# Second attention: the causal mask of a diagonal tile's row maximum, added by VectorE in the PSUM bank instead of by TensorE products

## The chip, the cores and the metric

One core of one Trainium2 chip runs the whole kernel. The metric is the device time of one execution in microseconds (us), the median of three runs. The program works on five engines that wait for each other through semaphores: TensorE (PE, with its weight loads PEld), VectorE (DVE), ScalarE (ACT), GpSimd (POOL) and SyncE (SP).

## What is computed

The reference has two layers, each an attention `s` times a gate `silu(g)`, added to `x`. The change is in the attention of the second layer, a causal softmax over 2048 positions with 16 heads of 64:

```python
scores = jnp.einsum('bqhd,bkhd->bhqk', q, k) / jnp.sqrt(jnp.float32(D_HEAD))
causal = jnp.tril(jnp.ones((seq, seq), dtype=bool))
scores = jnp.where(causal, scores, -jnp.inf)
pattern = jax.nn.softmax(scores, axis=-1)
z = jnp.einsum('bhqk,bkhd->bqhd', pattern, v)
attn_out = jnp.einsum('bqhd,hdm->bqm', z, W_O) + b_O
```

The softmax subtracts from each row an estimate of its maximum before the exponential. This maximum has to be taken over the columns that the causal mask leaves, and it is this mask that the change moves.

## The kernel before, in words

`attention1` works on 8 pairs of heads; the two heads of a pair lie in the lower and upper 64 partitions, called m = 0 and 1. For a pair, the queries are cut in 4 chunks of 512 columns (qc) and the keys in 16 tiles of 128 (kt). The main work is a list of 320 steps (pair, qc, kt) with kt up to the diagonal, so 4, 8, 12 and 16 steps for the four chunks of a pair, 40 for a pair. Four steps make a **group**, ten groups a **lap** (one pair).

All products that another engine has to read out go through **units**: a ring of RING = 3 places of two PSUM banks each. `UNIT` is the one hand-written order of all units, and TensorE, ScalarE and VectorE each walk it:

- `scores`: one step, a transposed 128 x 512 tile of scores for both heads. Six products for the scores in two precisions (L1788) and two that add minus the row maximum (L1791). ScalarE takes the exponential into `prob` (L1895) and so frees the place.
- `maximum`: one tile of 128 query rows i by up to 512 keys (chunk c), for the row maximum alone: one product per head, q_hi by k_hi (L1731). VectorE reduces it along the free axis into `part_max` (L1952), 128 x (2 x n) elements to 128 x 2, and so frees the place. There are 40 such tiles per pair, 320 in all; 16 per pair, 128 in all, are **diagonal** (c == i // 4) and are n = 128, 256, 384 or 512 columns wide per head, four of each per pair. In those the last 128 columns need the mask. Before, TensorE adds it: four products per tile (L1736, two per head, in bf16, 128 columns each) of an identity with a mask table, into the same bank.
- `project`, `value`, `turn`, `mix`: the projections of q, k and v for the next pair, the turn of the maxima into a row, and the output product. `turn` needs the maxima of its whole chunk (`neg_max`, L1960).

TensorE may fill the place of unit n only when unit n - 3 is freed (`room_for`). A group is: its rows phase (`rows_phase`: mostly a maximum, a scores, a maximum, a scores and so on, by the tables MAXIMA and PLACES), its whole phase (`whole_phase`: one to three of the other units), a `total` of the sums where a chunk has ended, and then the four `weigh` (L1810, prob by v, eight products, into a bank of their own), which need no place in the ring. VectorE walks the same units, and after a chunk has ended it also does `scale` (L1973 a reciprocal of 128 x 512, L1976 a product), behind the units of the group and ahead of those of the next. The maxima are computed ahead of the scores that need them: the first pair's in the start and groups 0 to 4, the others' in the 70 groups after that (seven equal laps), and the last five groups have none.

Where two VectorE instructions depend on each other, `link` (class Chain) makes the later wait on a semaphore that the earlier one raises at its end.

The mask table and the identity are made by GpSimd in `second_constants`, during the first attention.

Of the kernel before, what the change touches and what calls it, by code (L numbers as in the profile page):

```python
# [9 lines left out]
BF16 = mybir.dt.bfloat16  # L10
I32 = mybir.dt.int32
ALU = mybir.AluOpType
# [3 lines left out]
P = 128  # L16
# [3 lines left out]
C = 512  # L20
NC = S // C
TC = C // P
# [21 lines left out]
HD1 = 64  # L44
# [3 lines left out]
NEG = -1e30  # L48
# [344 lines left out]
def join_result(nc, link, sh, c, x_done):  # L393

    at = slice(c * TC, (c + 1) * TC)
    for t in range(c * TC, (c + 1) * TC):
        last = nc.gpsimd.tensor_scalar(sh.xa[:, t, 0:D], sh.xa[:, t, 0:D], sh.rstd[:, 0, t:t + 1],  # L397
                                       sh.shift[:, 0, t:t + 1], ALU.mult, ALU.add)
    link(last)
    link(nc.gpsimd.tensor_tensor(sh.xa[:, at, 0:D], sh.xa[:, at, 0:D], sh.g[:, at, :], ALU.mult))  # L400
    nc.gpsimd.tensor_tensor(sh.x[:, at, :], sh.x[:, at, :], sh.xa[:, at, 0:D], ALU.add).then_inc(x_done, 1)
# [30 lines left out]
def attention0(nc, a, sh):  # L432

    with ExitStack() as ctx:
# [7 lines left out]
        RING = 3  # L442
# [55 lines left out]
        @block.sync  # L498
        def _(sp):

            load_rows(sp, sh, 2, q_rows[2], k_rows[2], rows_loaded[2])
            load_rows(sp, sh, 3, q_rows[3], k_rows[3], rows_loaded[3])
            sp.dma_start(sh.w_out[:, :], a["L0_attn_w_out"]).then_inc(sh.join_loaded, 16)
            for n, name in enumerate(("b_out", "gamma", "beta")):
                sp.dma_start(sh.rows[:, n, :], a["L0_attn_" + name].partition_broadcast(P)).then_inc(sh.join_loaded, 16)
            for n, name in enumerate(("w_gate", "w_up")):
                sp.dma_start(sh.w_int[:, n, :].rearrange("p (t d) -> p t d", d=D),
                             a["L1_ffn_" + name].rearrange("(t p) d -> p t d", p=P)).then_inc(sh.join_loaded, 16)
            sp.dma_start(sh.w_int[:, 2, :], a["L1_ffn_w_down"]).then_inc(sh.join_loaded, 16)
            load_heads_start(sp, a, sh)  # L510

        @block.gpsimd
        def _(pool):
            link = Chain(pool, fold_step)

            def row(n):
                return sh.rows[:, n:n + 1, :].to_broadcast([P, T, D])

            for group in range(1, G):
                nc.gpsimd.memset(v_cols[group][:, :, :, HD0 + 1:VW], 0.0)  # L520
                nc.gpsimd.memset(v_cols[group][:, :, :, HD0:HD0 + 1], 1.0)
                heads = sh.v0[:, :, group * GH * HD0:(group + 1) * GH * HD0]
                nc.gpsimd.tensor_copy(v_cols[group][:, :, :, 0:HD0],
                                      heads.rearrange("p t (h j) -> p t h j", j=HD0)).then_inc(v_copied, 1)

            pool.wait_ge(sh.join_loaded, 16 * 7)
            link(nc.gpsimd.tensor_tensor(beta_g, sh.g[:, :, :], row(2), ALU.mult))
            link(nc.gpsimd.tensor_tensor(sh.x[:, :, :], sh.x[:, :, :], beta_g, ALU.add))
            link(nc.gpsimd.tensor_tensor(sh.g[:, :, :], sh.g[:, :, :], row(1), ALU.mult))
            link(nc.gpsimd.tensor_tensor(sh.xa[:, :, 0:D], sh.xa[:, :, 0:D], row(0), ALU.add))  # L530
            pool.sem_inc(folded, 1)

            second_constants(nc, link, sh, sh.xnT)

            for c in range(NC - 1):
                pool.wait_ge(scaled, 2 * c + 1)
                join_result(nc, link, sh, c, x_done)
                pool.wait_ge(scaled, 2 * c + 2)
                join_normal(nc, sh, c, normed)
# [921 lines left out]
                multiply(3, f)  # L1461


def second_constants(nc, link, sh, scratch):

    HALF = [slice(0, HD1), slice(HD1, 2 * HD1)]
    for m in range(2):
        masks = scratch[:, m * C:(m + 1) * C].rearrange("p (k h c) -> p k h c", k=2, h=2)
        link(nc.gpsimd.memset(masks, 0.0))
        link(nc.gpsimd.affine_select(out=masks[:, 0, :, :], in_=masks[:, 0, :, :], compare_op=ALU.is_ge,  # L1470
                                     fill=NEG, base=-m * HD1, pattern=[[HD1, 2], [-1, P]], channel_multiplier=1))
        link(nc.gpsimd.affine_select(out=masks[:, 1, :, :], in_=masks[:, 1, :, :],
                                     compare_op=ALU.not_equal, fill=1.0, base=-m * HD1,
                                     pattern=[[HD1, 2], [-1, P]], channel_multiplier=1))
        nc.gpsimd.tensor_copy(sh.causal[HALF[m], :, :], masks[HALF[m], 0, :, :])
        link(nc.gpsimd.tensor_copy(sh.ident_b[HALF[m], :, :], masks[HALF[m], 1, :, :]))
    nc.gpsimd.memset(sh.ones_r[:, :].bitcast(F32), 1.0)
    link(nc.gpsimd.memset(sh.own_tile[:, :, :], 0.0))
    for m in range(2):
        link(nc.gpsimd.affine_select(out=sh.own_tile[:, :, :], in_=sh.own_tile[:, :, :], compare_op=ALU.not_equal,  # L1480
                                     fill=1.0, base=-m * HD1, pattern=[[-1, TC], [0, P]], channel_multiplier=1))
# [15 lines left out]
def attention1(nc, a, sh, out):  # L1497

    with ExitStack() as ctx:
# [6 lines left out]
        W = HD1  # L1506
        HALF = [slice(0, W), slice(W, 2 * W)]
        NP = H // 2
        PR = 6
        RING = 3  # L1510
# [60 lines left out]

            return hp * NC + c

        wo, row_o, causal, ident_b, ones_r, own_tile = sh.wo, sh.row_o, sh.causal, sh.ident_b, sh.ones_r, sh.own_tile
        bias = sb("bias", [P, 3, NP])
        q_hi = sb("q_hi", [P, S], F32R)
        q_lo = sb("q_lo", [P, S], F32R)
        k_hi = [sb(f"k_hi{n}", [P, S], F32R) for n in range(2)]
# [37 lines left out]
        unit_both = [sh.psum[:, 2 * r:2 * r + 2, :] for r in range(RING)]  # L1616
# [84 lines left out]
        def _(pe):  # L1701
# [21 lines left out]
            def maximum(hp, i, c):  # L1723
                to = room_for(("maximum", hp, (i, c)))
                if c == 0 and i % TC == 0:

                    pe.wait_ge(act_split, (nth("project", hp, i // TC) + 1) * 2)
                n = min(C, (i + 1) * P - c * C)
                diagonal = c == i // TC
                for m in range(2):  # L1730
                    last = nc.tensor.matmul(to[:, m, 0:n], q_hi[HALF[m], i * P:(i + 1) * P],  # L1731
                                            k_hi[hp % 2][HALF[m], c * C:c * C + n], start=True, stop=not diagonal)
                if diagonal:
                    for half in range(2):
                        for m in range(2):
                            last = nc.tensor.matmul(to[:, m, n - P:n], ident_b[HALF[m], half, :],  # L1736
                                                    causal[HALF[m], half, :], start=False, stop=half == 1)
                last.then_inc(unit_filled, 1)

            def turn_maxima(hp, c):  # L1740
# [89 lines left out]
            for m in range(3):  # L1830
                last = nc.tensor.transpose(out_bank[:, m * NP:(m + 1) * NP], sh.bias_rows[:, m * P:(m + 1) * P],
                                           sh.ident[0:NP, 0:NP])
# [7 lines left out]
            for n in range(NP):  # L1840
                last = nc.tensor.matmul(side_bank[:, 0:D], bias_v[:, n, :], wo[:, n, :],
                                        start=n == 0, stop=n == NP - 1)
# [82 lines left out]
        def _(dve):  # L1925
            link = Chain(dve, result_step)
# [21 lines left out]
            def reduce_tile(hp, i, c):  # L1948
                n = AT["maximum", hp, (i, c)]
                cols = min(C, (i + 1) * P - c * C)  # L1950
                dve.wait_ge(unit_filled, n + 1)
                nc.vector.tensor_reduce(part_max[:, :, i, c], unit_both[n % RING][:, :, 0:cols], AX_X, ALU.max)\  # L1952
                    .then_inc(unit_freed[n % RING], 1)
                if (i + 1) % TC == 0 and c == i // TC:

                    tiles = [u for u in TILES if u[1] == hp and u[2][0] // TC == c]
                    for r in range(RING):
                        for u in [u for u in tiles if AT[u] % RING == r][-1:]:
                            wait_freed(dve, u)
                    nc.vector.tensor_reduce(neg_max[:, c % 2, :, 0:TC], part_max[:, :, c * TC:(c + 1) * TC, 0:c + 1],  # L1960
                                            AX_X, ALU.max, negate=True).then_inc(max_done, 1)
# [118 lines left out]
def build(nc, a, out):  # L2080
    with ExitStack() as ctx:
        sh = Shared()

        def sb(name, shape, dt=F32):
            return ctx.enter_context(nc.sbuf_tensor(name, shape, dt))
# [8 lines left out]
        sh.x_high, sh.x_low = (sb(name, [P, S], F32R) for name in ("x_high", "x_low"))  # L2094
        sh.wo = sb("wo", [P, H // 2, D])
        sh.row_o = sb("row_o", [P, D])
        sh.causal, sh.ident_b = (sb(name, [P, 2, P], BF16) for name in ("causal", "ident_b"))
        sh.ones_r = sb("ones_r", [P, P], F32R)
        sh.own_tile = sb("own_tile", [P, TC, P])
        sh.bias_rows = sb("bias_rows", [H // 2, 3 * P])  # L2100
# [62 lines left out]
```

## Time and profile before

| | before |
|---|---|
| median of 3 runs | 1413.13 us (1411.38 to 1413.79) |
| profiled execution | 1410.19 us |
| its span, first to last instruction | 1408.2 us |
| mean granted TensorE clock | 0.982 |
| busy: PE / DVE / ACT / POOL | 93% / 72% / 53% / 49% |
| second attention, from the start of the span | from about 548 us to the end |

The profile is one execution, seen by the hardware profiler. A line's busy time counts overlapping instructions once, the mean is that of one instruction. In a timeline each row is a run of equal instructions on one engine: start, length, engine, line, what is written from what, shape, count, and in brackets the idle time before it and whose end ended it. The products of the two heads of a unit run side by side in the halves of the array, so a pair of products of 512 columns starts every 0.23 us and not every 0.46.

### The profile page before, as it was taken

How to read it: one execution, taken by the hardware profiler on the slowest of the kernel's cores; microseconds unless marked ns; L12 is line 12 of the kernel's file. 1: busy time of each engine (PE TensorE's matmuls, PEld its weight loads, DVE VectorE, ACT ScalarE, POOL GpSimd, SP SyncE). 2: the span in 40 equal slices, each digit the busy share in tenths (PEclk: the TensorE clock that was granted, in tenths of full speed). 3: DMA queues.
4: the chain of work that ended last, by engine and by line, in shares of the span. 5: the costliest groups of instructions: out<-in, count | busy, mean ns of one | idle time of the engine just before them, and what ended most of it. 6: DMA issues, size and time to landing. Idle time of an engine off the chain costs nothing.

```text
span 1408.2 us, 25489 instructions
## 1 busy us (share of the span) xinstructions
PE 1313.0 (93%) x9902; PEld 674.9 (48%) x9902; DVE 1015.9 (72%) x1495; ACT 749.8 (53%) x1200; POOL 691.9 (49%) x527
## 2 busy tenths in 40 slices
PE   5778999999999987989999999999999999999897
PEld 3654222222222245555555655555555555555554
DVE  7666888888888875776766766766766666766768
ACT  5275777877777774334444444444344344344343
POOL 4301060100100010558678678677677677777671
PEclk9799999999999999999999999999999999999999
DMA  2511320000000000000000000000000000000000
GB/s 98 160 74 51 111 47 1 1 1 1 2 1 2 2 1 1 1 1 1 1 1 1 1 1 1 1 1 0 1 1 1 1 1 1 1 1 1 1 16 16
DMA packets 18166, 21.50 MB, mean 15 GB/s; under 512 B 7785, under 2 KB 15873, under 8 KB 16513
## 3 DMA queue, kind: packets, MB, share of 16 engines
q1 hardware_dynamic: 18048, 19.88, 4.6%
q8 instruction: 81, 1.33, 0.4%
q14 instruction: 37, 0.30, 0.1%
HBM read 14.63 MB, written 5.24 MB: 14 GB/s over the span
## 4 chain that ended last, share of the span: by engine, by line
PE 43%; DVE 11%; ACT 3%; issue 1%; POOL 1%; DVEq 0%; POOLq 0%; ACTq 0%
PE psum L1810 13%; PE psum L1788 12%; DVE part_max L1952 4%; PE psum L1731 4%; DVE inv L1973 4%; PE psum L1791 3%; ACT prob L1895 3%; PE psum L1769 2%; PE psum L1718 2%; PE psum L1757 2%; PE psum L1709 1%; DVE z L1976 1%; PE psum L1711 1%; PE psum L1710 1%; PE psum L1736 1%
## 5 line engine op out<-in xcount | busy, mean ns | idle before, releaser
L1698 POOL TENSOR_TENSOR acc<-acc,prob 128x1024 f32<-128x1024 f32 (+3 forms) x250 | 492.8, 1971 | 87.4 <-ACT prob L1895 57.6
L1895 ACT ACTIVATE prob<-psum 128x1024 f32<-128x1024 f32 (+1 forms) x320 | 283.3, 897 | 353.8 <-PE psum L1791 346.4
L1952 DVE TENSOR_REDUCE part_max<-psum 128x2 f32<-128x1024 f32 (+2 forms) x320 | 336.7, 1063 | 170.0 <-PE psum L1731 85.6
L696 DVE TENSOR_SCALAR w<-psum 128x512 f32<-128x512 f32 x472 | 304.7, 686 | 59.0 <-PE psum L553 46.6
L647 ACT ACTIVATE w<-psum 128x512 f32<-128x512 f32 x552 | 294.2, 600 | 85.4 <-PE psum L553 84.8
L573 PE MATMUL psum<-w,v_cols 128*32 128x512 f32 x2048 | 274.1, 608 | 0.0
L1810 PE MATMUL psum<-prob,v_pair 128*64 128x512 f32 (+3 forms) x1280 | 250.2, 532 | 0.7 <-POOL prob L1666 0.7
L1788 PE MATMUL psum<-q_hi,k_hi 64*128 64x512 f32 (+3 forms) x640 | 139.0, 430 | 30.4 <-DVE part_max L1952 21.5
L1810 PEld LDWEIGHTS psum<-prob,v_pair 128*64 128x64 f32 x1280 | 87.4, 137 | 145.2 <-issue 134.2
L1731 PE MATMUL psum<-k_hi,q_hi 64*128 64x512 f32 (+3 forms) x640 | 132.5, 411 | 6.0 <-DVE part_max L1952 4.4
L1788 PE MATMUL psum<-q_lo,k_hi 64*128 64x512 f32 (+3 forms) x640 | 119.1, 368 | 0.0
L1788 PE MATMUL psum<-q_hi,k_lo 64*128 64x512 f32 (+3 forms) x640 | 119.1, 368 | 0.0
L1791 PE MATMUL psum<-max_rows,ones_r 64*128 64x512 f32 (+3 forms) x640 | 118.7, 366 | 0.0
L1973 DVE RECIPROCAL inv<-psum 128x512 f32<-128x512 f32 x31 | 103.9, 3352 | 16.5 <-PE psum L1757 16.5
L553 PEld LDWEIGHTS psum<-q_rows,k_rows 32*128 32x128 f32 x768 | 40.3, 181 | 154.0 <-ACT w L647 148.1
L397 POOL TENSOR_SCALAR xa<-xa,rstd_j,shift_j 128x128 f32<-128x128 f32 x16 | 6.9, 449 | 209.0 <-DVE shift_j L389 209.0
L1666 POOL TENSOR_SCALAR_AFFINE_SELECT prob<-prob 128x256 f32<-128x256 f32 x128 | 53.3, 423 | 110.9 <-ACT prob L1895 110.1
L553 PE MATMUL psum<-q_rows,k_rows 32*128 32x512 f32 x768 | 101.6, 493 | 0.1
L1788 PEld LDWEIGHTS psum<-q_hi,k_hi 64*128 64x128 f32 x640 | 61.4, 188 | 78.0 <-DVE part_max L1952 47.4
L1731 PEld LDWEIGHTS psum<-k_hi,q_hi 64*128 64x128 f32 x640 | 61.2, 187 | 77.6 <-issue 40.8
L1694 POOL TENSOR_TENSOR acc<-prob 128x1024 f32<-128x1024 f32 x23 | 54.9, 2385 | 43.2 <-ACT prob L1895 41.4
L573 PEld LDWEIGHTS psum<-w,v_cols 128*32 128x32 f32 x2048 | 40.6, 108 | 63.8 <-ACT w L647 53.5
(301 smaller groups left out, 1411.3 us busy)
## 6 DMA issues: line engine op xcount, KB each, us to landing
q_rows<-q_dram SPq DMA_DIRECT2D x12, 256.0 KB
k_rows<-k_dram SPq DMA_DIRECT2D x3, 1024.0 KB
q_dram<-parts SPq DMA_DIRECT2D x2, 1024.0 KB, 4.2
k_dram<-parts SPq DMA_DIRECT2D x2, 1024.0 KB, 6.6
x<-in_L_attn_x SPq DMA_DIRECT2D x4, 256.0 KB, 4.0
mask<-in_L_ffn_attention_mask SPq DMA_DIRECT2D x1, 1024.0 KB, 6.0
x_high<-q_dram SPq DMA_DIRECT2D x4, 256.0 KB
x_low<-k_dram SPq DMA_DIRECT2D x1, 1024.0 KB
```

The lines of the kernel that those rows point to most:

```text
L553: last = nc.tensor.matmul(pair_bank[n % RING][i], k_rows[group][rows, kt * P:(kt + 1) * P], q_rows[group][rows, qc * C:(qc + 1) * C], star ...
L573: last = nc.tensor.matmul(out_bank[turn % 2][h * VW:(h + 1) * VW, :], v_cols[group][:, kt, h, :], w[:, s % WR, h, :], start=(kt == 0), sto ...
L647: nc.scalar.activation(w[:, s % WR, 2 * m + i, :], pair_bank[n % RING][i], ACT.Relu)\
L696: nc.vector.tensor_scalar(w[:, s % WR, 2 * m + 1, :], pair_bank[n % RING][1], 0.0, None, ALU.max)\
L1698: nc.gpsimd.tensor_tensor(sums, sums, prob[:, s % PR, :, q0:C], ALU.add).then_inc(summed, 1)
L1731: last = nc.tensor.matmul(to[:, m, 0:n], q_hi[HALF[m], i * P:(i + 1) * P], k_hi[hp % 2][HALF[m], c * C:c * C + n], start=True, stop=not di ...
L1788: nc.tensor.matmul(to[:, m, q0:C], left[HALF[m], keys], right[HALF[m], at], start=n == 0, stop=False)
L1791: last = nc.tensor.matmul(to[:, m, q0:C], ones_r[HALF[m], :], max_rows[HALF[m], at], start=False, stop=True)
L1810: last = nc.tensor.matmul(out_bank[HALF[m], q0:C], v_pair[hp % 2][:, kt, HALF[m]], prob[:, s % PR, m, q0:C], start=kt == 0, stop=kt == (qc ...
L1895: nc.scalar.activation(prob[:, s % PR, :, q0:C], unit_both[n % RING][:, :, q0:C], ACT.Exp, scale=SCALE)\
L1952: nc.vector.tensor_reduce(part_max[:, :, i, c], unit_both[n % RING][:, :, 0:cols], AX_X, ALU.max)\
L1973: nc.vector.reciprocal(inv[:, :], side_bank).then_inc(inv_done, 1)
```

## The change

The four mask products of a diagonal tile (L1736) are gone; the tile's two products then close their accumulation themselves. In their place VectorE, when it comes to a diagonal tile, first adds a mask of 128 x 128 f32 (zero, or -1e30 above the diagonal) to the last 128 columns of both banks, in place in PSUM, for both heads in one instruction, waits for its end through `link`, and then runs the reduce as before. The mask table is one f32 tile in place of two pairs of bf16 ones, and the identity is gone; `second_constants` has a memset and a select in place of ten instructions.

```diff
-def second_constants(nc, link, sh, scratch):
...
+    link(nc.gpsimd.memset(sh.causal[:, :], 0.0))
+    link(nc.gpsimd.affine_select(out=sh.causal[:, :], in_=sh.causal[:, :], compare_op=ALU.is_ge, fill=NEG, base=0,
+                                 pattern=[[-1, P]], channel_multiplier=1))
...
                 for m in range(2):
                     last = nc.tensor.matmul(to[:, m, 0:n], q_hi[HALF[m], i * P:(i + 1) * P],
-                                            k_hi[hp % 2][HALF[m], c * C:c * C + n], start=True, stop=not diagonal)
-                if diagonal:
-                    for half in range(2):
-                        for m in range(2):
-                            last = nc.tensor.matmul(to[:, m, n - P:n], ident_b[HALF[m], half, :],
-                                                    causal[HALF[m], half, :], start=False, stop=half == 1)
+                                            k_hi[hp % 2][HALF[m], c * C:c * C + n], start=True, stop=True)
...
                 dve.wait_ge(unit_filled, n + 1)
+                if c == i // TC:
+                    own = unit_both[n % RING][:, :, cols - P:cols]
+                    link(nc.vector.tensor_tensor(own, own, causal[:, :].unsqueeze(1).to_broadcast([P, 2, P]), ALU.add))
                 nc.vector.tensor_reduce(part_max[:, :, i, c], unit_both[n % RING][:, :, 0:cols], AX_X, ALU.max)\
                     .then_inc(unit_freed[n % RING], 1)
...
-        sh.causal, sh.ident_b = (sb(name, [P, 2, P], BF16) for name in ("causal", "ident_b"))
+        sh.causal = sb("causal", [P, P])
```

On VectorE, around the end of chunk 3 of a pair's scores (groups 16 and 17), the instructions stood in this order before (the reduces of `maximum` units are `part_max<-psum`; x5 means five in a row):

```order
L1960 TENSOR_REDUCE neg_max<-part_max 128x2x4
L1952 TENSOR_REDUCE part_max<-psum 128x2 x3
L1941 SCALAR_TENSOR_TENSOR k_lo0<-psum,bias,k_hi0 128x512
L1944 SCALAR_TENSOR_TENSOR q_lo<-psum,bias,q_hi 128x512
L1973 RECIPROCAL inv<-psum 128x512
L1976 TENSOR_TENSOR z<-z,inv 128x512
L1952 TENSOR_REDUCE part_max<-psum 128x2 x5
```

and so they stand now:

```order
L1949 TENSOR_REDUCE neg_max<-part_max 128x2x4
L1941 TENSOR_REDUCE part_max<-psum 128x2
L1940 TENSOR_TENSOR psum<-psum,causal 128x2x128
L1941 TENSOR_REDUCE part_max<-psum 128x2 x2
L1927 SCALAR_TENSOR_TENSOR k_lo0<-psum,bias,k_hi0 128x512
L1930 SCALAR_TENSOR_TENSOR q_lo<-psum,bias,q_hi 128x512
L1962 RECIPROCAL inv<-psum 128x512
L1965 TENSOR_TENSOR z<-z,inv 128x512
L1940 TENSOR_TENSOR psum<-psum,causal 128x2x128
L1941 TENSOR_REDUCE part_max<-psum 128x2 x2
L1940 TENSOR_TENSOR psum<-psum,causal 128x2x128
L1941 TENSOR_REDUCE part_max<-psum 128x2 x2
```

Each diagonal tile has one add more, straight ahead of its reduce, and one of them stands directly behind the reciprocal and product of `scale`.

On TensorE, at the end of group 14 (tiles of query rows 15 by keys of chunk 3), the order was

```order
L1791 MATMUL psum<-max_rows,ones_r 128x512 x2
L1731 MATMUL psum<-k_hi0,q_hi 128x512 x2
L1736 MATMUL psum<-causal,ident_b 128x128 x4
L1709 MATMUL psum<-x_high,w_high 128x512
L1710 MATMUL psum<-x_low,w_high 128x512
```

and is now

```order
L1777 MATMUL psum<-max_rows,ones_r 128x512 x2
L1722 MATMUL psum<-k_hi0,q_hi 128x512 x2
L1701 MATMUL psum<-x_high,w_high 128x512
L1702 MATMUL psum<-x_low,w_high 128x512
```

The four mask products have gone, and nothing else has moved.

## Rows read from the trace of the kernel before

**Rows 1.** The page: busy time by engine, and one group of GpSimd.

```profile
PE 1313.0 (93%) x9902; PEld 674.9 (48%) x9902; DVE 1015.9 (72%) x1495; ACT 749.8 (53%) x1200; POOL 691.9 (49%) x527
...
L397 POOL TENSOR_SCALAR xa<-xa,rstd_j,shift_j 128x128 f32<-128x128 f32 x16 | 6.9, 449 | 209.0 <-DVE shift_j L389 209.0
```

**Rows 2.** Stretches: from:to, length, engines' busy us (instructions), clock, DMA share, GB/s.

```profile
717.50:822.50 105.00, 101.09 (x735) 60.11 (x733) 69.71 (x69) 45.22 (x56) 79.60 (x54) 0.98 0.00 1
822.50:926.30 103.80, 99.88 (x736) 59.03 (x734) 69.86 (x70) 45.19 (x56) 79.42 (x54) 1.00 0.00 1
...
794.70:798.10 3.40, 3.40 (x18) 2.50 (x16) 2.03 (x3) 1.97 (x2) 2.15 (x1) 0.51 0.00 0
```

**Rows 3.** Groups by line and shape, 520 to 1408: busy us, mean ns | idle before.

```profile
L1952 DVE TENSOR_REDUCE part_max<-psum 128x2 f32<-128x1024 f32 x224 | 272.2, 1223 | 93.6 <-PE psum L1731 85.6 <-PE psum L1736 6.7
...
L1736 PE MATMUL psum<-causal,ident_b 64*128 64x128 bf16 x512 | 36.9, 222 | 0.0
...
L1967 DVE TENSOR_TENSOR max_rows<-psum,own_tile 128x512 fp32r<-128x512 f32 x32 | 21.8, 682 | 13.5 <-PE psum L1743 13.5
...
L1952 DVE TENSOR_REDUCE part_max<-psum 128x2 f32<-128x256 f32 x32 | 13.6, 425 | 17.4 <-PE psum L1736 15.9
```

**Rows 4.** Who waited for whom, whole span: us in total, times, longest us.

```profile
PEld psum L1788 <- DVE part_max L1952: 47.4, 80, 2.3
```

**Rows 5.** Timeline of group 14 behind the end of a chunk, DVE and PE.

```profile
717.38 3.35 DVE L1973 RECIPROCAL inv<-psum 128x512 f32<-128x512 f32 x1
...
720.77 0.69 DVE L1976 TENSOR_TENSOR z<-z,inv 128x512 f32<-128x512 f32 x1
...
721.38 2.08 DVE L1952 TENSOR_REDUCE part_max<-psum 128x2 f32<-128x768 f32 x2
...
722.38 0.50 PE L1788 MATMUL psum<-q_hi,k_hi 64*128 64x512 f32 x2 [0.93 <-DVE part_max L1952]
```

**Rows 6.** Timeline of PE in groups 16 and 17.

```profile
740.58 0.41 PE L1731 MATMUL psum<-k_hi,q_hi 64*128 64x512 f32 x2
...
740.91 0.49 PE L1788 MATMUL psum<-q_hi,k_hi 64*128 64x512 f32 x2
741.23 0.41 PE L1788 MATMUL psum<-q_hi,k_lo 64*128 64x512 f32 x2
...
742.43 0.50 PE L1788 MATMUL psum<-q_hi,k_hi 64*128 64x512 f32 x2
...
745.18 0.50 PE L1709 MATMUL psum<-x_high,w_high 128*128 128x512 f32 x1
...
756.21 0.39 PE L1731 MATMUL psum<-k_hi,q_hi 64*128 64x512 f32 x2
756.44 0.41 PE L1788 MATMUL psum<-q_hi,k_hi 64*128 64x512 f32 x2
756.69 0.40 PE L1788 MATMUL psum<-q_hi,k_lo 64*128 64x512 f32 x2
```

**Rows 7.** Timeline of DVE in groups 16 and 17.

```profile
739.81 0.96 DVE L1952 TENSOR_REDUCE part_max<-psum 128x2 f32<-128x768 f32 x1 [2.12 <-PE psum L1736]
741.15 1.23 DVE L1952 TENSOR_REDUCE part_max<-psum 128x2 f32<-128x1024 f32 x1 [0.39 <-PE psum L1736]
...
742.50 1.78 DVE L1952 TENSOR_REDUCE part_max<-psum 128x2 f32<-128x1024 f32 x2
...
752.91 0.68 DVE L1952 TENSOR_REDUCE part_max<-psum 128x2 f32<-128x512 f32 x1
```

**Rows 8.** Timeline of DVE in group 11, behind the end of a chunk.

```profile
688.44 1.21 DVE L1952 TENSOR_REDUCE part_max<-psum 128x2 f32<-128x1024 f32 x1
```

**Rows 9.** Timeline of DVE at the start of the second attention.

```profile
553.13 3.01 DVE L1952 TENSOR_REDUCE part_max<-psum 128x2 f32<-128x256 f32 x4
...
558.84 0.29 DVE L2050 TENSOR_TENSOR row_o<-row_o,psum 128x128 f32<-128x128 f32 x1 [1.23 <-PE psum L1841]
```

**Rows 10.** Timeline of PE in group 21, one lap after group 11.

```profile
793.59 0.50 PE L1788 MATMUL psum<-q_hi,k_hi 64*128 64x512 f32 x2 [1.87 <-DVE part_max L1952]
```

More of the change, by code:

```diff
@@ L531, in _ @@
             pool.sem_inc(folded, 1)
-            second_constants(nc, link, sh, sh.xnT)
+            second_constants(nc, link, sh)
             for c in range(NC - 1):
@@ L1461, in _, with second_constants @@
                 multiply(3, f)
-def second_constants(nc, link, sh, scratch):
-    HALF = [slice(0, HD1), slice(HD1, 2 * HD1)]
-    for m in range(2):
[L1468 to L1476, printed above, removed]
+def second_constants(nc, link, sh):
+    link(nc.gpsimd.memset(sh.causal[:, :], 0.0))
+    link(nc.gpsimd.affine_select(out=sh.causal[:, :], in_=sh.causal[:, :], compare_op=ALU.is_ge, fill=NEG, base=0,
+                                 pattern=[[-1, P]], channel_multiplier=1))
     nc.gpsimd.memset(sh.ones_r[:, :].bitcast(F32), 1.0)
@@ L1572, in nth @@
             return hp * NC + c
-        wo, row_o, causal, ident_b, ones_r, own_tile = sh.wo, sh.row_o, sh.causal, sh.ident_b, sh.ones_r, sh.own_tile
+        wo, row_o, causal, ones_r, own_tile = sh.wo, sh.row_o, sh.causal, sh.ones_r, sh.own_tile
         bias = sb("bias", [P, 3, NP])
@@ L1728, in maximum @@
                 n = min(C, (i + 1) * P - c * C)
-                diagonal = c == i // TC
                 for m in range(2):
                     last = nc.tensor.matmul(to[:, m, 0:n], q_hi[HALF[m], i * P:(i + 1) * P],
-                                            k_hi[hp % 2][HALF[m], c * C:c * C + n], start=True, stop=not diagonal)
-                if diagonal:
-                    for half in range(2):
-                        for m in range(2):
-                            last = nc.tensor.matmul(to[:, m, n - P:n], ident_b[HALF[m], half, :],
-                                                    causal[HALF[m], half, :], start=False, stop=half == 1)
+                                            k_hi[hp % 2][HALF[m], c * C:c * C + n], start=True, stop=True)
                 last.then_inc(unit_filled, 1)
```

## The prediction

> **What bounds the kernel now.** The page comes first: TensorE is busy in 93% of the span and VectorE in 72% [rows 1], so a change that takes work from the one and gives it to the other looks like a gain. The stretches say the same of a single lap: in 103.80 us TensorE is busy 99.88 and VectorE 69.86 [rows 2]. But the busy share hides latencies: a matmul's row counts its pass through the array. The waits must be read. The weight loads of the scores waited 47.4 us in 80 places for VectorE's reduce of a maximum [rows 4], nearly all in the stretches where the work is passed to and fro through the ring of three places. And the timelines show the kind: a scores unit starts 0.05 us after the reduce three units before it has ended (reduce ends at 742.38, next scores at 742.43 [rows 6, 7]). So in a rows phase the time is often set by fill, reduce, fill, exponential, and only in the whole phase and the weigh by TensorE's own stream. What counts is which diagonal tiles lie on that chain.
>
> **What TensorE saves.** The 512 mask products occupy 36.9 us [rows 3], 0.29 per tile, but they overlap their neighbours. What goes is read from starts. With a mask, from the tile's first product to the second pair of the scores behind it is 741.23 - 740.58 = 0.65 us; without one, in a stretch where nothing waits, 756.69 - 756.21 = 0.48 [rows 6]. So a tile gives back about 0.17 us, where TensorE is the last; 0.10 is the low end (the start alone: 740.91 - 740.58 = 0.33 against 0.23). For 128 tiles that is 13 to 22 us, if all were on the path. Where the unit behind the mask waits for the ring anyway, it gives nothing. Weighed against the trace, the Trainium skill (TensorE: Matmul & The Clock Gate, section "Back-to-back issue gap") has a stream of loads and products of 128 columns spaced about 81 ns apart, which would make four of them 324 ns a tile and the whole 41 us; the starts above are closer together, since the two heads' products run side by side.
>
> **What VectorE gains in work.** One add of 128 x 256 elements, PSUM and SBUF in, PSUM out. The trace has no such write to PSUM; the nearest rows are the add from PSUM and SBUF of 128 elements, 0.29 us [rows 9], and the product of 512, 682 ns [rows 3]: in between, 0.42 for 256, which is also what a reduce of 256 takes (425 ns [rows 3]). To that comes the wait of the reduce for the add: 0.04 us, as between the reciprocal (ends 720.73) and the product that waits for it (starts 720.77) [rows 5]. I take 0.46 per tile, 59 us in all. The ends: 0.40, and, if a write into PSUM cost as much again as the fixed part of the shortest row, 0.6. The skill says (VectorE: DVE Perf Modes, section "The DRAIN you can't avoid") that the semaphore costs nothing extra between chained instructions. Four reduces without a wait take 3.01 us for 0.43 + 0.69 + 0.96 + 1.22 = 3.30, that is, they overlap by about 0.1 [rows 9]; a waiting one does not. By the page's rule 0.14 us of each exposed add would go, some 6 us of the sum.
>
> Queued behind the add and its wait on VectorE are the reduce of the same tile, then the next tiles, the low halves of the projections, and `scale`. For the reduce waits TensorE's unit three places on.
>
> **Which tiles expose it.** I walk one lap (groups 11 to 20), 16 diagonal tiles, unit by unit, from the start of each unit, the end of the reduce or exponential three units before, and what is next late.
>
> - Behind `scale`, three places per lap. VectorE comes out of reciprocal and product late, has a tile waiting, and TensorE waits for it: reduces start at 688.44, 721.38 and 752.91 [rows 5, 7, 8]; the scores two units on wait 0.93 us in group 14 (start 722.38, [rows 5]) and 1.87 in group 21, a lap after group 11 [rows 10]. The full 0.46 goes on the path, in the first two places for good. In the third (group 17) two more diagonal tiles, of 384 and 512 columns, follow; the exponentials had been late there and TensorE's saving counts, which leaves about 0.25. Together 1.17.
> - Group 16: tiles of 384 and 512 columns one behind the other. The scores at 740.91 started 0.15 after the first reduce had ended (739.81 + 0.96 = 740.77 [rows 6, 7]). The tile is filled 0.13 earlier, the reduce ends 0.34 later, at 741.11, so that scores starts at 741.17. The second reduce (741.15 to 742.38) then ends at 741.11 + 0.46 + 1.23 = 742.8, and the scores of 742.43 start at 742.87. The third, of 128 columns, ends at about 745.1 in place of 744.28 and is covered (the projection starts at 745.18, by then 745.56). Net 0.38. Group 20, one of 384 columns with three short scores behind it, goes the same way through the exponentials: 0.36. Together 0.74.
> - Tiles of 128 and 256 columns, six of them elsewhere: their reduce is 0.8 to 0.5 shorter than that of a full tile, so the add fits under the same cover, and the mask products stood before a unit that waited for the ring. Zero either way. If that cover were gone, 0.46 each.
> - TensorE last: a 512 tile ahead of a projection in group 14 and a 128 tile at the start of group 15. They give back 0.10 and 0.15, so -0.25.
>
> A lap gains 1.17 + 0.74 - 0.25 = 1.66 us; seven laps 11.6. The weigh phases between do not absorb it: they run on TensorE's own stream and start when it is there. The first pair's maxima are read in the same way: four diagonal tiles back to back before any scores, 553.13 to 556.14 [rows 9], with the turn waiting behind: 4 x 0.46 = 1.9. Groups 0 to 4, where two maxima stand between scores, give about 1.0, 0, 0.6, 0.1 and 0.5. Together about 4.
>
> **The clock.** In one of the two laps shown the granted clock falls to half for 3.4 us (0.51, its 1.2 GHz level, at 794.70 to 798.10) right behind the longest stall (1.87 us, group 21); the lap with the fall takes 105.00, that without 103.80 [rows 2, 10], so a fall costs 1.2 us. The stall grows to 2.3 us, in every lap. I count two falls more than before, 2 us.
>
> **What is removed on GpSimd** lies in the first attention, before a row that idles 209.0 us for VectorE [rows 1]. Zero. The instruction order of nothing else changes.
>
> **The sum.** 11.6 + 4 + 2 = 17.6 us. On the profiled execution that is 1410.2 + 17.6 = 1427.8; the median of the runs lies 2.9 higher, and on it I forecast 1413.1 + 17.6 = 1430.7. The mechanism's own range: only the two places behind `scale` that stay and the start (0.92 - 0.25 per lap, 2 for the first pair) give +7, to 1420; an add of 0.6 and two more exposed tiles per lap (5.5 x 0.14 + 2 x 0.46 = 1.7 a lap, 12 in all) give +30, to 1443.
>
> **Rivals.**
> - *TensorE is the bound after all (faster).* Place: every diagonal tile. VectorE idles 34 us of a lap [rows 2], and the add goes there; each tile gives back 0.10 to 0.17. 1413.1 less 13 to 22: 1391 to 1400. It decides if, in most tiles, the unit three on starts over 0.35 us after the reduce has ended. For it speaks the 93%, against it the 0.05 and 0.93 above. By the page's 81 ns it would be 1372. Chance 0.08 for both.
> - *It comes out even.* The exposed tiles' loss is as large as the gain at tiles that I hold to be covered: 10 tiles a lap at 0.15 against 1.66 and less clock loss, within 3 us of 1413. Chance 0.05.
> - *More is exposed.* All eight tiles of 384 and 512 columns a lap pay 0.46 (3.7 a lap, 29 in all, with 2 for the clock): 1444. For it: full tiles already cost VectorE 1.22 each [rows 3], against five pairs of products at 0.23 = 1.15 of TensorE for a maximum with its scores. Chance 0.12. That all 128 pay, +59, 1472: 0.02.
> - *The add is dearer than thought.* At 0.7 us (+0.24 in some 46 exposed places): +11 more, 1442. Chance 0.05, in the range.
>
> The forecast's mechanism has the rest, 0.68. What a measurement of this kernel can tell from no change is about 0.2%, 2.8 us. Faster 0.08, same 0.05, slower 0.87. The range 1419 to 1445 leaves out the faster and even cases, the extreme one, and little else.
>
> **What would show it.** After: the add near 0.42 us in 128 places, and the reduce 0.04 behind it; waits of PE for the reduce up from 47.4 us on the weight loads; laps of 105.5 to 106.7 us; the scores behind `scale` start 0.46 later from the start of the lap; the stall of 1.87 becomes 2.3; six to seven falls of the clock in the second attention. It would be wrong if the laps are shorter than 103.8, if the add takes 0.6 or more, if the small tiles expose it, or if the clock falls as often as before.

## The result and the profile after

| | before | after |
|---|---|---|
| median | 1412.26 us (4 runs) | 1430.53 us (1429.16 to 1433.12, 4 runs) |
| ratio | | 1.0134, 95% interval 1.0119 to 1.0149 |
| profiled execution, its span | 1410.19, 1408.2 | 1433.12, 1431.2 |
| mean granted clock in it | 0.982 | 0.976 |

The change makes the kernel 18.3 us slower; 17.6 were forecast (1430.7 us). The profiled execution is the slowest of the four, so its trace holds some 2 to 3 us more than the median.

Busy time moved as the edit says. The page of after, its first part:

```profile
PE 1308.5 (91%) x9390; PEld 667.4 (47%) x9390; DVE 1068.8 (75%) x1623; ACT 749.5 (52%) x1200; POOL 688.6 (48%) x519
```

TensorE lost 512 products and 4.5 us of busy time [rows 1], VectorE got 52.9 us more. The new group among the lines and shapes of the second attention, beside the reduce whose mean has not changed [rows 3]:

```profile
L1941 DVE TENSOR_REDUCE part_max<-psum 128x2 f32<-128x1024 f32 x224 | 272.4, 1224 | 70.4 <-PE psum L1722 67.9
...
L1940 DVE TENSOR_TENSOR psum<-psum,causal 128x256 f32<-128x256 f32 x128 | 54.9, 429 | 69.0 <-PE psum L1722 67.4
```

The add takes 429 ns. The waits show who pays (us in total, times, the longest; the first line is of the trace of before, the others of after):

```profile
PE psum L1788 <- DVE part_max L1952: 21.5, 27, 1.9
```

```profile
PEld psum L1774 <- DVE part_max L1941: 82.0, 107, 3.0
...
PE psum L1774 <- DVE part_max L1941: 41.3, 58, 2.5
```

The loads of the scores waited 47.4 us for the reduce [rows 4] and now wait 82.0; the scores' products waited 21.5 and now wait 41.3. Group 14, the same place as [rows 5], one group after the end of a chunk:

```profile
727.19 3.35 DVE L1962 RECIPROCAL inv<-psum 128x512 f32<-128x512 f32 x1
...
730.57 0.69 DVE L1965 TENSOR_TENSOR z<-z,inv 128x512 f32<-128x512 f32 x1
...
731.18 0.42 DVE L1940 TENSOR_TENSOR psum<-psum,causal 128x256 f32<-128x256 f32 x1
731.64 2.09 DVE L1941 TENSOR_REDUCE part_max<-psum 128x2 f32<-128x768 f32 x2
...
732.66 0.50 PE L1774 MATMUL psum<-q_hi,k_hi 64*128 64x512 f32 x2 [1.58 <-DVE part_max L1941]
```

From the start of the reciprocal to that of the scores it was 722.38 - 717.38 = 5.00 us, and it is 732.66 - 727.19 = 5.47: the add and its wait, whole. And group 16, with two tiles behind one another:

```profile
749.69 0.43 DVE L1940 TENSOR_TENSOR psum<-psum,causal 128x256 f32<-128x256 f32 x1 [1.99 <-PE psum L1722]
...
750.16 0.96 DVE L1941 TENSOR_REDUCE part_max<-psum 128x2 f32<-128x768 f32 x1
...
751.17 0.50 PE L1774 MATMUL psum<-q_hi,k_hi 64*128 64x512 f32 x2 [0.35 <-DVE part_max L1941]
751.49 1.23 DVE L1941 TENSOR_REDUCE part_max<-psum 128x2 f32<-128x1024 f32 x1
```

The first reduce ends at 751.12 and the scores start at 751.17. Before, that scores had started 0.15 after its reduce, when TensorE was ready [rows 6, 7].

A lap without any loss of clock, from the start of group 60 to that of group 70, took 103.86 us before and takes 105.63 (from:to, length, engines' busy us, clock, DMA share, GB/s; the first row is of the trace of before, the second of after):

```profile
1200.51:1304.37 103.86, 99.94 (x734) 58.97 (x732) 69.80 (x69) 45.21 (x56) 79.67 (x54) 1.00 0.01 1
```

```profile
1220.04:1325.67 105.63, 98.49 (x670) 57.26 (x668) 76.42 (x85) 45.12 (x56) 79.68 (x54) 1.00 0.00 1
```

So the lap is 1.77 us longer; 1.66 were forecast. By group, from the starts of the same units in both traces (median over the six laps of groups 11 to 70):

| group of the lap | 11 | 12, 13 | 14 | 15 | 16 | 17 | 18, 19 | 20 |
|---|---|---|---|---|---|---|---|---|
| forecast, us | +0.46 | 0 | +0.36 | -0.15 | +0.38 | +0.25 | 0 | +0.36 |
| measured, us | +0.53 | 0 | +0.33 | -0.12 | +0.32 | +0.36 | +0.06 | +0.33 |

The clock often falls to half in the first group of a lap (11, 21 and so on), so the median of that column mixes laps with a fall and laps without. Between laps of the same clock it is +0.50 (14.34 us before and 14.84 after without a fall, 15.6 and 16.1 with one). The stall in front of the scores there, 1.87 us before [rows 10], is 2.54 and not the 2.3 of the forecast, since TensorE also comes to it 0.2 us sooner, without its four products.

The largest part that the forecast missed is the start. From the first projection to the first unit of group 0 the changed kernel takes 3.98 us more, where 1.9 were forecast, and by group 5 it is 6.4 more, where about 4 were. Timeline of TensorE there, first before and then after (the sixteen products mix the bias and do not depend on the mask):

```profile
556.59 0.30 PE L1743 MATMUL psum<-ident,neg_max 128*128 128x128 f32 x1 [1.23 <-DVE neg_max L1960]
556.72 2.01 PE L1841 MATMUL psum<-wo,prob 128*128 128x128 f32 x16
```

```profile
559.44 0.45 PE L1729 MATMUL psum<-ident,neg_max 128*128 128x128 f32 x1 [2.21 <-DVE neg_max L1949]
559.68 3.64 PE L1827 MATMUL psum<-wo,prob 128*128 128x128 f32 x16
```

The second attention itself starts 0.61 later in this execution (its first projection at 548.52, before at 547.91), so the turn is late by 559.44 - 556.59 - 0.61 = 2.24. The four adds are 1.87 of it (the last of the four reduces ends at 558.62, before at 556.14); the rest, 0.37, is a longer pause between that reduce and `neg_max`, which stays open. Another 1.63 us are the same sixteen products, which took 2.01 and take 3.64. The stretch of 546 to 563 us has a granted clock of 0.99 before and 0.81 after:

```profile
546.00:563.00 17.00, 11.71 (x91) 8.89 (x91) 10.27 (x15) 7.12 (x10) 0.72 (x2) 0.99 0.01 1
```

```profile
546.00:563.00 17.00, 11.33 (x61) 9.11 (x59) 8.24 (x14) 4.82 (x8) 0.31 (x1) 0.81 0.01 1
```

These two rows overstate the difference: the kernel before has a fall of its own, 3.4 us from 562.5 on, just outside. Over 546 to 580 us the clock is 0.95 before and 0.85 after. Nor does one trace show that the adds made those products slow, as the last of the experiments tells. Where the clock was at half after the start, in this execution: two spells up to the end of group 0 (6.8 and 3.4 us; before one of 3.4), and seven spells of 3.4 us in groups 11 to 78 where before had four. Five of the seven start in or right behind the stall of groups 11, 21 and so on, before all four.

### The profile page after: what moved, and what is told of

Same layout as the page of the kernel before. It is cut to its first block, busy times and chain, and to the rows that moved or that the text cites. A ratio compares the mean times of both kernels' runs of the same rounds, so it can differ in the third digit from the quotient of the medians.

```text
span 1431.2 us, 24582 instructions
## 1 busy us (share of the span) xinstructions
PE 1308.5 (91%) x9390; PEld 667.4 (47%) x9390; DVE 1068.8 (75%) x1623; ACT 749.5 (52%) x1200; POOL 688.6 (48%) x519
## 4 chain that ended last, share of the span: by engine, by line
PE 37%; DVE 19%; ACT 3%; POOL 1%; issue 1%; DVEq 0%; POOLq 0%; ACTq 0%
PE psum L1796 11%; PE psum L1774 10%; DVE part_max L1941 8%; DVE inv L1962 5%; PE psum L1722 3%; PE psum L1777 3%; ACT prob L1881 2%; PE psum L1755 2%; PE psum L1710 2%; DVE psum L1940 2%; PE psum L1701 1%; DVE z L1965 1%; PE psum L1743 1%; POOL acc L1690 1%; PE psum L1703 1%; PE psum L1702 1%
## 5 line engine op out<-in xcount | busy, mean ns | idle before, releaser
L1774 PE MATMUL psum<-q_hi,k_hi 64*128 64x512 f32 (+3 forms) x640 | 136.5, 423 | 52.5 <-DVE part_max L1941 41.3
L1940 DVE TENSOR_TENSOR psum<-psum,causal 128x256 f32<-128x256 f32 x128 | 54.9, 429 | 69.0 <-PE psum L1722 67.4
```

The source lines that it names most:

```text
L1774: nc.tensor.matmul(to[:, m, q0:C], left[HALF[m], keys], right[HALF[m], at], start=n == 0, stop=False)
```

## The experiments

The theory under test, here the chain theory: a mask step costs its time only at a tile that stands in the chain of ring and VectorE. Its rivals: every add costs the same share (18.3 / 128 = 0.14 us), TensorE is the bound, or most of the loss is clock. All ratios are against the kernel before on the same chip (medians 1409.84 for the first four kernels below, no mask to narrow; 1410.53 for behind scale, first pair, the add set aside and TensorE last; 1410.45 for later pairs and the two with the product on GpSimd). Differences in us are of medians.

Where a kernel masks some tiles with one engine and some with the other, the edit to the kernel before is one condition (and a table `mask_v` beside the old ones, made by GpSimd at the start of the second attention):

```diff
+def by_vector(hp, i, c):
+    return ...                      # the condition named with the run
+
+
+def by_tensor(hp, i, c):
+    return not by_vector(hp, i, c)
...
-                diagonal = c == i // TC
+                diagonal = c == i // TC and by_tensor(hp, i, c)
...
+                if c == i // TC and by_vector(hp, i, c):
+                    own = unit_both[n % RING][:, :, cols - P:cols]
+                    link(nc.vector.tensor_tensor(own, own, mask_v[:, :].unsqueeze(1).to_broadcast([P, 2, P]), ALU.add))
```

**No mask.** The changed kernel without its add:

```diff
-                if c == i // TC:
-                    own = unit_both[n % RING][:, :, cols - P:cols]
-                    link(nc.vector.tensor_tensor(own, own, causal[:, :].unsqueeze(1).to_broadcast([P, 2, P]), ALU.add))
```

> The changed kernel without the add on VectorE: no mask is put on the row maxima at all, by neither engine, so the maximum of a diagonal tile is taken over unmasked columns. It measures what TensorE's four products per tile were worth by themselves. Chain theory (a mask step costs only where its tile is in the chain of ring and VectorE): each lap gains about 0.9 us against the kernel before, mostly because the fill of a diagonal tile ends 0.13 us sooner in groups 16, 17 and 20, and the start about 1: 1412.3 - 7 = 1405. TensorE-bound rival: 0.10 to 0.17 us at every one of 128 tiles: 1390 to 1399. Rival that the products were wholly hidden: 1412, no change.

Measured: 1405.53 us, ratio 0.9965 (0.9954 to 0.9977), so -4.3. TensorE's products were worth a third of a per cent, not the 13 to 22 us of the rival. Between laps of the same clock its lap is 1.1 us shorter than before (0.13 to 0.31 each in groups 14 to 17, 19 and 20). The clock is lower than before (0.978 or 0.979 in six of the seven runs, 0.984 in one, against a mean of 0.983). Its trace has a spell at half clock over the sixteen products of the start:

```profile
546.00:563.00 17.00, 12.01 (x71) 9.46 (x70) 8.80 (x13) 5.90 (x9) 0.31 (x1) 0.90 0.01 1
```

But that is the spell of the kernel before, of the same 3.4 us, come sooner (at 556.4 and not 562.5): over 546 to 580 us both have 0.95.

```profile
546.00:580.00 34.00, 26.86 (x180) 19.00 (x179) 21.89 (x28) 14.52 (x21) 8.42 (x10) 0.95 0.00 1
```

```profile
546.00:580.00 34.00, 27.84 (x218) 19.77 (x216) 22.54 (x29) 15.09 (x21) 8.97 (x10) 0.95 0.01 1
```

(The first row is of this kernel, the second of the one before.) So the start does not show that the missing products cost clock; the mean clock of the runs says that the kernel as a whole has lost some, and where stays open.

**Both masks.** TensorE's products and VectorE's add in every diagonal tile (`by_vector` and `by_tensor` true everywhere).

> Both masks: TensorE's four products and VectorE's add in every diagonal tile (the mask is added twice, which changes no result). It measures the add by itself. Chain theory: the loss of the change, 18.3, and what the products' removal had given back, 7: 1437 to 1438. If the products' removal gave nothing: 1430.5. If VectorE's work counted as a sum, 128 x 0.46 = 59 us: 1471.

Measured: 1439.32 us, ratio 1.0205 (1.0185 to 1.0224), +29.5. The lap is 2.8 us longer, against 1.8 with the change. So the removal of the products does give something back at the same places, some 1.0 of the 2.8 a lap. As a sum VectorE's work (128 x 0.46 = 59) is twice what is lost.

**Wide and narrow tiles.** `by_vector` is `i % TC >= 2` (384 and 512 columns) in the first, `i % TC < 2` (128 and 256) in the second; 64 adds each.

> VectorE adds the mask in the diagonal tiles of 384 and 512 columns (64 of 128), TensorE in those of 128 and 256. Chain theory: nearly all of the loss is here, 7 laps x 1.6 + 2 in the first pair + 2 of clock = 15: 1427 to 1428. Even-share rival (each add costs 18.3 / 128 = 0.14 us wherever it stands): 1421.4.

> The complement: VectorE adds the mask in the diagonal tiles of 128 and 256 columns, TensorE in those of 384 and 512. Chain theory: only the tile behind scale in group 17, 0.2 a lap, less 0.15 in group 15, and 1.6 in the first pair: 1412.3 + 2 = 1414. Even-share rival: 1421.4.

Measured: wide 1428.36 us, ratio 1.0144 (1.0114 to 1.0174); narrow 1415.97 us, ratio 1.0043 (1.0028 to 1.0058). +18.5 and +6.1, not 9 and 9: the even share falls. (One of the four runs of wide, the profiled one, took 1436.56 at a clock of 0.971, the others 1427 to 1429.) By the groups of a lap, wide adds 1.6 us, as worked out, and narrow 0.20 (0.24 in group 17, -0.13 in group 15, 0.07 in group 19), where 0.05 were worked out. Narrow missed its expectation: +6.1 for about +2. Its lap explains 1 us of that; the clock has the most of the rest (table below).

**Behind scale only.** `hp >= 1 and (i, c) in ((5, 1), (11, 2), (14, 3))`, 21 adds.

> VectorE adds the mask in only 21 tiles, the three per lap whose reduce stands directly behind scale's reciprocal and product (query rows 5 of chunk 1, 11 of chunk 2, 14 of chunk 3, pairs 1 to 7); TensorE in the other 107. Chain theory: 0.46 + 0.46 + 0.2 = 1.1 a lap, 7.8 in all, and up to 1 of clock: 1420 to 1421. Even-share rival, 21 x 0.14 = 3.0: 1415.3.

Measured: 1418.80 us, ratio 1.0064 (1.0051 to 1.0078): +8.3 from 21 adds, 0.39 each, where the other 107 of the change bring 10. This separates the chain theory from the even share (3.0) at one stroke. The groups: +0.39, +0.46, +0.25 in 11, 14 and 17 (in group 11 +0.48 between laps of the same clock). The clock is that of the kernel before, 0.983 in three of four runs, though the stall of group 11 has grown from 1.87 to 2.54 us.

**The first pair only**, `hp == 0`, and its complement, `hp >= 1`.

> VectorE adds the mask only in the first pair's 16 diagonal tiles. The start of group 0 came 3.4 us later there against the start of the attention in the changed kernel, where I had worked out 1.9, and by group 5 it was 6.4 later where I had 4; the granted clock was at half for 6.8 us in that stretch against 3.4 before. Chain theory with the clock: 4 from the chain, 1 to 3 from the clock: 1416.5 to 1419. Chain theory alone: 1416.3. Even-share rival, 16 x 0.14: 1414.6.

> The complement of the run with the first pair only: VectorE adds the mask in the 112 diagonal tiles of pairs 1 to 7, TensorE keeps the first pair's 16. It tells where the lost clock of the change comes from. In the runs so far a kernel whose first pair is changed has a mean granted clock of 0.974 to 0.980, the kernel before 0.983, and the two kernels that leave the first pair alone 0.983. Chain theory, clock lost in the first pair's stretch only: 7 laps x 1.8 = 12.6 on 1410.5: 1423, at a clock of 0.982 to 0.983. If the longer stalls of the laps cost the clock: 1425 to 1427, at 0.979 or 0.980.

Measured: the first pair 1417.67 us, ratio 1.0054 (1.0040 to 1.0067), clock 0.977 to 0.980; the later pairs 1423.22 us, ratio 1.0085 (1.0064 to 1.0105), clock 0.982 to 0.984. So 16 adds cost 7.1 us and the 112 others 12.8. All four runs with VectorE's masks in the first pair have a lower clock than the four with TensorE's there (they ran on two chips; the kernel before has a mean of 0.983 on both). The traces put the loss at the start: with TensorE's masks, 546 to 580 us has

```profile
546.00:580.00 34.00, 28.00 (x217) 20.02 (x215) 21.96 (x28) 14.51 (x21) 8.82 (x12) 0.95 0.00 1
```

and with VectorE's

```profile
546.00:580.00 34.00, 25.72 (x139) 19.02 (x139) 22.07 (x33) 10.96 (x17) 7.18 (x11) 0.75 0.00 1
```

or 17.0 us at half against 3.4, while in groups 11 to 78 both have four falls, as many as the kernel before. The lap of the later pairs' kernel is longer by 1.8, as in the change, and its mean clock stays.

**The add set aside.** It writes to a tile in SBUF that nobody reads, and nothing waits for it:

```diff
-                    link(nc.vector.tensor_tensor(own, own, causal[:, :].unsqueeze(1).to_broadcast([P, 2, P]), ALU.add))
+                    nc.vector.tensor_tensor(aside[:, i % 8, :, :], own, causal[:, :].unsqueeze(1).to_broadcast([P, 2, P]),
+                                            ALU.add)
```

> The changed kernel, but the add writes its result to a tile in SBUF that nobody reads, and the reduce does not wait for it: the mask does not reach the maximum. It measures what the write into PSUM and the wait between add and reduce cost. Chain theory with the price as I took it: the add itself stays 0.43 us, but add and reduce overlap by 0.1 instead of standing 0.04 apart, so 0.14 less in some 46 to 50 exposed places: 1430.5 - 7 = 1423 to 1424. If the wait costs nothing: 1430.5. If the write into PSUM were dear, the add's row here would be well below 429 ns.

Measured: 1425.19 us, ratio 1.0106 (1.0091 to 1.0122), 3.9 us below the change by the ratios. The add's mean is 420 ns against 429, so with PSUM as destination it takes 9 ns more:

```profile
L1941 DVE TENSOR_TENSOR aside<-psum,causal 128x256 f32<-128x256 f32 x128 | 53.8, 420 | 69.5 <-PE psum L1723 67.3
```

The lap is 0.74 longer than before where the change's is 1.81, so the wait between add and reduce is worth 1.07 a lap or 7.5 in all, a little more than I took. Per tile it is about 0.12 us: with it the reduce starts 0.035 behind the add's end, without it 0.083 ahead of it (medians of the two traces). Nearly half of the 7.5 was lost to the clock, whose mean is the lowest of all kernels here (0.972 to 0.976); in this trace it is at half for 10 us in a row in group 0, as it is in that of the first pair only. Why is open.

**TensorE last.** `hp >= 1 and (i, c) in ((0, 0), (15, 3)) or (hp, i, c) == (0, 15, 3)`, 15 adds, where I had found TensorE the last and VectorE under cover.

> VectorE adds the mask only in 15 tiles, those at which I found TensorE last and VectorE under cover (rows 0 of chunk 0, pairs 1 to 7, and rows 15 of chunk 3, all pairs); TensorE does the other 113. Chain theory: -0.25 a lap, so 1412.3 - 1.8 = 1410.5, if the clock falls as often as before. Even-share rival, 15 x 0.14 = 2.1: 1414.4.

Measured: 1407.96 us (12 runs), ratio 0.9985 (0.9976 to 0.9995). The same edit that costs 0.39 us a tile behind `scale` gains 0.12 at each of two places of a lap (groups 14 and 15, -0.12 each). It is smaller than 0.2%, but its interval excludes 1.

**The product of scale on GpSimd.** All this says that the place behind `scale` is on the path, so what stands ahead of the tile there was taken away, in the kernel before and in the last one:

```diff
             def scale(g):
                 dve.wait_ge(totalled, g + 1)
+                if g:
+                    dve.wait_ge(scaled, g)
                 nc.vector.reciprocal(inv[:, :], side_bank).then_inc(inv_done, 1)
-                dve.wait_ge(inv_done, g + 1)
-                dve.wait_ge(z_copied, g + 1)
-                nc.vector.tensor_tensor(z[:, g % 2, :], z[:, g % 2, :], inv[:, :], ALU.mult).then_inc(scaled, 1)
...
+            def scale_z(g):
+                pool.wait_ge(inv_done, g + 1)
+                pool.wait_ge(z_copied, g + 1)
+                nc.gpsimd.tensor_tensor(z[:, g % 2, :], z[:, g % 2, :], inv[:, :], ALU.mult).then_inc(scaled, 1)
...
+                if s - 5 in CHUNK_LAST:
+                    scale_z(CHUNK_LAST.index(s - 5))
```

> The kernel before, with one move that the rows behind scale point to: the product of scale (z by the reciprocal, 0.69 to 1.17 us on VectorE, 31 times) goes to GpSimd, behind the fourth step after the chunk's end; VectorE keeps the reciprocal, and waits ahead of the next one until GpSimd has used the last. Chain theory: the tile behind scale starts 0.7 to 1.2 us sooner in groups 11, 14 and 17, of which TensorE was waiting 1.87, 0.93 and 0.1 or so: -1.2, -0.7, -0.1 to -0.3 a lap, 2.1 in all, 15 us on seven laps: 1395. Rival (GpSimd, at 77% of a lap already, becomes late with the sums, for which the exponentials wait): 1411 or slower.

> The same move to GpSimd in the kernel in which VectorE adds the mask at 15 tiles and TensorE at the other 113 (which was 2.6 us faster than the kernel before). Chain theory: the two gains add up, 1395 - 2 = 1393. Rival as above: 1409 or slower.

Measured: 1392.56 us, ratio 0.9868 (0.9845 to 0.9890), and with the 15 adds 1391.59 us, ratio 0.9863 (0.9840 to 0.9886). Both beat the kernel before and the changed one; the two are not told apart from each other. Group 11 of the first, GpSimd, TensorE and VectorE:

```profile
689.34 1.28 POOL L1672 TENSOR_TENSOR z<-z,inv 128x512 f32<-128x512 f32 x1
689.84 0.50 PE L1795 MATMUL psum<-q_hi,k_hi 64*128 64x512 f32 x2 [0.61 <-DVE part_max L1959]
```

and the same scores in the timeline of the change:

```profile
698.16 0.50 PE L1774 MATMUL psum<-q_hi,k_hi 64*128 64x512 f32 x2 [2.54 <-DVE part_max L1941]
```

TensorE's stall is 0.61 there, where it was 1.87 a lap later in the kernel before [rows 10] and 2.54 with the change. GpSimd does the product in 1313 ns, and no exponential waits for its sums. Group 14 is 0.79 shorter, group 17 no shorter, where I had 0.1 to 0.3. Group 11 is 1.25 shorter against laps of before in which the clock had not fallen, and 2.5 against those in which it had: in or right behind that stall the clock fell in four of the seven laps before (4 of 7 too with the first pair only and with behind scale only, 3 with later pairs, 5 with the change), and in none of the seven of either kernel with the product on GpSimd. So 2.04 us a lap, 14.3 in all, are the chain, 15 were expected, and most of what was gained beyond is clock.

This trace also tells something of the start, where the kernel runs the code of before up to group 1:

```profile
556.83 3.64 PE L1848 MATMUL psum<-wo,prob 128*128 128x128 f32 x16
```

```profile
546.00:563.00 17.00, 13.42 (x87) 10.58 (x85) 8.81 (x13) 5.35 (x9) 0.31 (x1) 0.80 0.01 1
```

The sixteen products take 3.64 us, as in the change, without any add of VectorE. Of the six kernels that start with the code of before this is the one trace with slow products; the seven others all have them slow (2.4 to 3.6 us). So the slow products go with a changed start (no mask, or adds of VectorE), but are not tied to it: the unchanged code had them too in this execution.

**The price of clock.** Every run lists its mean granted clock; the time at half clock is twice the span times what the clock lacks to 1. Over all 93 runs of the twelve kernels and of the kernel before, each kernel against its own mean, a microsecond more at half clock goes with 0.28 us more time (correlation 0.89), so 3.4 us at half with 0.96. This is a regression, no experiment of its own. With it the difference of each kernel's mean to that of the kernel before (1410.4 us in 34 runs, 47.7 us at half clock) splits:

| kernel | difference | at half clock, us | by clock | rest | chain theory |
|---|---|---|---|---|---|
| change | +20.5 | 62 | 4.1 | +16.4 | +15.6 |
| no mask | -5.4 | 57 | 2.7 | -8.1 | -7 |
| both | +28.3 | 64 | 4.6 | +23.7 | +23 |
| wide | +19.7 | 66 | 5.3 | +14.4 | +13 |
| narrow | +5.5 | 61 | 3.7 | +1.8 | +2 |
| aside | +14.6 | 73 | 7.2 | +7.4 | +9 |
| behind scale | +8.7 | 50 | 0.5 | +8.2 | +7.8 |
| first pair | +7.2 | 61 | 3.7 | +3.5 | +4 |
| later pairs | +12.4 | 49 | 0.4 | +12.0 | +12.6 |
| TensorE last | -2.1 | 48 | 0.0 | -2.2 | -1.8 |
| product on GpSimd | -18.3 | 39 | -2.5 | -15.8 | -15 |
| both moves | -18.9 | 42 | -1.7 | -17.2 | -17 |

(The change ran on another chip. Against the mean of before there, 1412.3, its difference is 18.7 and its rest would be 14.6; the clock of those runs of before is known for one alone. The theory's column is the expectation without its allowance for clock.)

## Why the prediction was right

- *What bounds the kernel.* Right. The busy shares (93% and 72%) spoke for the change; the wait of the scores for the reduce spoke against it, and grew from 47.4 to 82.0 us.
- *What TensorE saves.* 0.10 to 0.17 us where it is the last, nothing where the next unit waits, unless the reduce itself then ends sooner: without masks groups 16, 17 and 20 are 0.31, 0.25 and 0.14 shorter. The no-mask run gives 8 us without the clock's part, where 7 were expected, and the run with both masks shows the same from the other side.
- *The price of the add.* 0.42 + 0.04 taken; 429 ns measured, and reduce behind add at 731.64 - 731.18 = 0.46. That PSUM as a destination costs next to nothing (9 ns) was unknown before and inside the range. The wait for the add is not free: without it the lap is 1.07 us shorter. The Trainium skill (VectorE: DVE Perf Modes, "The DRAIN you can't avoid") says that the semaphore costs nothing extra between chained instructions. This case does not agree: by that sentence the run with the add set aside would have been equal to the change.
- *Which tiles expose it.* Right group by group. Two terms were a little off (group 17 +0.36 for 0.25, group 16 +0.32 for 0.38), the narrow tile of group 19 costs 0.07 for 0, and the sum is 1.77 for 1.66 a lap.
- *The first pair.* The chain part holds, as far as the regression separates it: 3.5 without the clock's part, for 4.
- *The clock.* Near in size, in part by luck, and not borne out in its reason. The term was two more falls, 2 us, from the longer stalls of the laps. What 7 x 1.77 = 12.4 and 3.5 leave of the 18.3 is 2.4; the regression gives 4.1. But with the same longer stalls (2.54 us) the kernel of the later pairs keeps the clock of before (49 us at half against 48), and the one with the first pair alone loses 13 us: over the runs the loss is the first pair's, for which I had put nothing. The step that does not hold is "The stall grows to 2.3 us, in every lap. I count two falls more". In the one trace of the change the laps do have three falls more (seven for four), one of them at that stall; whether this is chance, and why the first pair costs clock, stays open. A stall cut to 0.61 us did take the falls at it away.
- *GpSimd's constants.* Zero, as said.

## What to carry to other kernels

Where units pass through a short ring between engines, the price of an instruction is not its duration times its count but a matter of place: the same 0.46 us cost 0.39 per tile behind a long VectorE block, 0.07 or nothing in a narrow tile elsewhere in the lap, and the move gained 0.12 where TensorE was last. Walk the units one by one, with the end of the release three units before beside each start, before moving work from a busy engine to an idle one. And look for what stands ahead of the exposed place: moving that to the engine with room there (here a product, to GpSimd) gained 18 us, seven times what the best choice of masks did.

## What the runs showed of the hardware

- A VectorE add of 256 elements per partition with PSUM as destination takes 429 ns, with SBUF as destination 420.
- A VectorE instruction that waits for the semaphore of the one ahead starts 0.04 us after its end (reduce behind add, 128 times in the change); without the wait it starts about 0.08 before (the add set aside). At exposed places this made 1.07 us a lap.
- The clock of a kernel can depend on which engine does a small piece of work at one place: 0.977 to 0.980 in four runs with VectorE's masks in the first pair, 0.982 to 0.984 in four with TensorE's there (0.983 for the kernel before on either chip). One trace does not place such a loss: the same code took 2.01 us for sixteen products in one execution and 3.64 in another.
- The longest stall of a lap can grow from 1.87 to 2.54 us without any loss in the mean granted clock (0.983 in both, behind scale only). With the stall cut to 0.61 us the clock fell there in no lap of seven, where it had fallen in four. Such a fall costs about 1.25 us (group 11: 15.6 against 14.34).
- GpSimd does a product of 128 x 512 f32 in SBUF in 1313 ns.
